# TensorE's table reads in the routed tiles of a fused Mamba and mixture-of-experts kernel: one per tile, ahead of the down products, the weight offset computed

## The reference

```
scores = softmax(x @ gate_w.T)            # 16 experts
topk_w, topk_ids = top_k(scores, 6)       # normalised to sum 1
y_e = (silu(x @ g_e.T) * (x @ u_e.T)) @ w2_e.T      # hidden 352
out = sum over the six chosen e of weight * y_e, + shared expert (hidden 704)
x = x + tanh(g_ffn) * out
```

## Time and profile before

| | us |
|---|---|
| median of three runs | 1439.65 |
| lowest and highest run | 1438.64, 1913.43 |
| span of the profiled execution, first to last instruction | 1435.5 |
| median less that span | 4.15 |
| TensorE products busy | 1349.9 (94%) |
| GpSimd busy | 949.3 (66%) |
| VectorE busy | 787.5 (55%) |
| ScalarE busy | 730.9 (51%) |

### The profile page before, as it was taken

The page is one execution under the profiler, slowest core; times in us unless marked ns, Lnnn a source line. Parts: engine busy times, 40 slices in busy tenths (PEclk is TensorE's granted clock), DMA queues, the critical chain, the costliest instruction groups (busy, mean ns, idle before and its releaser), DMA issues.

```text
span 1435.5 us, 32257 instructions
## 1 busy us (share of the span) xinstructions
PE 1349.9 (94%) x8480; PEld 1210.6 (84%) x8481; DVE 787.5 (55%) x1364; ACT 730.9 (51%) x1317; POOL 949.3 (66%) x671
## 2 busy tenths in 40 slices
PE   6897998997898899999999999999999999999996
PEld 2686887887888799999998989989889988899885
DVE  6878898898989854653333333333333333333331
ACT  5898897898889464343332333323333333332321
POOL 0588898898988747887456665566645666546632
PEclk8899999999999999999999999999999999999999
DMA  4120122222242365645455435555445544454432
GB/s 137 38 74 31 53 67 96 67 73 91 75 146 72 133 129 106 142 84 141 83 141 145 131 63 144 139 147 137 104 94 137 141 135 104 95 147 131 76 68 36
DMA packets 65042, 149.13 MB, mean 104 GB/s; under 512 B 16976, under 2 KB 17616, under 8 KB 62656
## 3 DMA queue, kind: packets, MB, share of 16 engines
q0 software_dynamic: 31024, 62.10, 22.9%
q1 hardware_dynamic: 33392, 81.21, 17.5%
q10 hardware_dynamic: 560, 4.98, 1.0%
HBM read 101.50 MB, written 48.99 MB: 105 GB/s over the span
## 4 chain that ended last, share of the span: by engine, by line
PE 65%; DVE 3%; issue 1%; POOL 0%; ACT 0%; DVEq 0%; POOLq 0%; ACTq 0%
PE bank L1719 19%; PE bank L1699 19%; PE bank L1700 18%; PE bank L1687 3%; PE bank L1710 3%; DVE hs L1172 1%; PE bank L1604 1%; PE bank L1590 1%; PE bank L1602 0%; POOL hc L949 0%; DVE sc L1226 0%; PE bank L1665 0%; DVEq L1375 0%; DVE xl L1363 0%; DVE du L1186 0%
## 5 line engine op out<-in xcount | busy, mean ns | idle before, releaser
L949 POOL TENSOR_TENSOR hc<-hs,crow 128x512 f32<-128x512 f32 x254 | 322.6, 1302 | 91.8 <-DVE hs L1172 84.6
L1699 PE MATMUL bank<-w,xh 128*128 (+1 forms) x1088 | 368.7, 340 | 7.6 <-issue 4.2
L1015 POOL DMA_INDIRECT out_x<-ys,aid x104 | 171.2, 1646 | 275.0 <-issue 215.7
L1700 PE MATMUL bank<-w,xh 128*128 (+1 forms) x1088 | 351.2, 323 | 0.0
L1172 DVE TENSOR_TENSOR_SCAN hs<-dA,bank 128x512 f32<-128x512 f32 x256 | 295.8, 1208 | 47.9 <-PE bank L1604 32.0
L1719 PE MATMUL bank<-w,ah 128*128 (+1 forms) x816 | 264.7, 405 | 2.7 <-DVE al L1399 2.7
L1399 DVE TENSOR_TENSOR al<-bank,ah 128x384 fp32r<-128x384 f32 x136 | 75.8, 557 | 331.0 <-ACT ah L862 283.2
L1699 PEld LDWEIGHTS bank<-w,xh 128*128 128x128 f32 x1088 | 204.3, 188 | 35.9 <-issue 32.1
L1700 PEld LDWEIGHTS bank<-w,xh 128*128 128x128 f32 x1088 | 206.4, 190 | 2.3
L868 ACT COPY ys<-bank 128x512 f32<-128x512 f32 x136 | 79.9, 587 | 195.9 <-PE bank L1719 191.5
L1700 PE MATMUL bank<-w,xl 128*128 (+1 forms) x544 | 175.9, 323 | 0.0
(11 more groups left out here) (184 smaller groups left out, 2051.7 us busy)
## 6 DMA issues: line engine op xcount, KB each, us to landing
wraw<-in_wall SPq DMA_DIRECT2D x16, 2176.0 KB
crow<-c_rows SPq DMA_DIRECT2D x64, 256.0 KB, 3.3
xt<-token_rows_turned SPq DMA_DIRECT2D x32, 256.0 KB
out_x<-ys POOLq DMA_DIRECT2D x32, 256.0 KB
wraw<-in_wall ACTq DMA_DIRECT2D x2, 2176.0 KB
token_rows<-rowb SPq DMA_DIRECT2D x4, 1028.0 KB
xrow<-in_x SPq DMA_DIRECT2D x4, 1024.0 KB, 7.0
out_x<-xrow SPq DMA_DIRECT2D x4, 1024.0 KB, 4.9
```

The lines of the kernel that those rows point to most:

```text
L949: nc.gpsimd.tensor_tensor(hc[:, j, :], hs[:, j, :], crow[:, n % 4, :], ALU.mult).then_inc(hc_done, 1)
L1015: pool.indirect_dma_start(out_rows, bass.IndirectOffsetOnAxis(ap=aid[:, s:s + 1], axis=0), ys[:, s, :], None, bounds_check=TOKENS - 1, oob ...
L1699: nc.tensor.matmul(gate_bank[:, 0:I], xx, columns(w, off + ww + k * 2 * I, I), start=first, stop=last)
L1700: mm = nc.tensor.matmul(up_bank[:, 0:I], xx, columns(w, off + ww + k * 2 * I + I, I), start=first, stop=last)
```

## The change

TensorE reads only row 0 of the table. For the second, third and fourth tile of a turn, the read stands at the end of the tile before, between `turn_x` and `down`; for the first tile of a turn it stands at the turn's head, together with a read of the number of the tile before. The offset is worked out in registers from the number: `(number + 1) % 2 * (2 * WCOLS)`, once for each tile of the turn and once for the tile before it. The wait for `wl_done` stays ahead of the up products. Reads of the table by TensorE go from nine to five per turn. The last tile, outside the loop, is treated in the same way.

```diff
-            def weights_of(t):
-                needed = pe.value_load(meta[0:1, 0, bass.ds(t, 1)], min_val=1, max_val=NX)
-                apart(pe, wl_done, needed, "pe")
-                return pe.value_load(meta[0:1, 1, bass.ds(t, 1)], min_val=0, max_val=2 * WCOLS)
-
-            def tile(t, s4, old, off, more=True, m=None):
+            def set_number(t):
+                return pe.value_load(meta[0:1, 0, bass.ds(t, 1)], min_val=1, max_val=NX)
+
+            def offset_of(number):
+                return pe.snap((number + 1) % 2 * (2 * WCOLS))
+
+            def tile(t, s4, old, off, more=True, m=None, ahead=None):
...
                     turn_x(t + 1, (s4 + 1) % 4, m)
-                down(t - 1, 1 - s, old() if callable(old) else old)
+                number = set_number(ahead) if ahead is not None else None
+                down(t - 1, 1 - s, old)
+                return number
...
             with pe.Fori(0, groups) as i:
-                def old():
-                    return pe.value_load(meta[0:1, 1, bass.ds(4 * i + PEELED - 1, 1)], min_val=0, max_val=2 * WCOLS)
-
+                number = set_number(4 * i + PEELED)
+                old = offset_of(set_number(4 * i + PEELED - 1))
                 for k in range(4):
-                    off = weights_of(4 * i + PEELED + k)
-                    tile(4 * i + PEELED + k, (3 + k) % 4, old, off, True, i)
+                    off = offset_of(number)
+                    apart(pe, wl_done, number, "pe")
+                    number = tile(4 * i + PEELED + k, (3 + k) % 4, old, off, True, i, 4 * i + PEELED + k + 1 if k < 3 else None)
                     old = off
             last = tiles_but_12(pe) + 11
-
-            def of_last(k):
-                return pe.value_load(meta[0:1, 1, bass.ds(last - k, 1)], min_val=0, max_val=2 * WCOLS)
-
-            tile(last, 3, lambda: of_last(1), weights_of(last), False)
+            number = set_number(last)
+            old, off = offset_of(set_number(last - 1)), offset_of(number)
+            apart(pe, wl_done, number, "pe")
+            tile(last, 3, old, off, False)
             turn_a(last, 1)
-            down(last, 1, of_last(0))
+            down(last, 1, off)
```

## The result

The changed kernel takes 1430.89 us in the median of five runs (1428.72 to 1434.58), the kernel before 1438.64 in five; the ratio is 0.9947, 95% interval 0.9934 to 0.9959. That is 0.5% faster, some 7.7 us, where 1443, slower by 3, was forecast, in a range that began at 1433. A second measurement of the same code (the first experiment) gives 0.9962, 0.9948 to 0.9975. One run of the kernel before, 1913.43, counts in its median and not in the ratio.

The account below looks back on a forecast made before the run. TensorE was taken to bound the routed stage, with 20.3 us of pauses at tile boundaries. Terms: -9.0 inner boundaries, +11.3 turn heads, +1.0 slower reads, sum +3.3 us, time 1443; range 1433 to 1453.

Parts of the forecast that it names:

- The bound and the pool: Routed stage: TensorE sets the pace; its pauses at 104 tile boundaries hold 20.3 us, all that can be won there.
- the 15 late tiles: Tiles where ScalarE and VectorE also split the next weights and activations come late; said to hold 10.3 of 20.3 us.
- (a): 78 inner boundaries: two reads give way to one computed offset; 9.0 us won, between 7.6 and 13.0.
- (b): Read moved ahead of the down products: costs nothing, taking 0.7 to 1.4 of 2.4 us in which the sequencer waits.
- The queue's fill: TensorE's queue behind the moved read; the only ground given for R3.
- (c): Head of each turn, 27 times: two computed offsets added on the path, 0.42 us each time, 11.3 us lost (6.5 to 20.5).
- (d): Loop turns: with inner gaps closed, about six more turns have a first read slowed by the gather; 1.0 us lost.
- R1: Rival: inner gaps close wholly, 13.0 us won, offsets cheap at 6.5 + 1.0 paid; 1434 us, chance 0.22.
- R2: Rival: at the turn's head each offset takes three or four instructions; 13.5 us slower, 1453 us, chance 0.20.
- R3: Rival: the moved read isn't hidden and delays down products by some 0.4 us in 78 tiles; 1474 us, chance 0.03.
- R4: Rival: late xl, not the reads, ended the gaps everywhere; inner boundaries win 2 instead of 9, 1450 us, chance 0.05.
- the case that had 0.95: Whole kernel: measured time the same within about 2% (29 us); faster had 0.01, slower 0.04.

Follow-up runs that it names:

- the first experiment: The changed kernel measured again with no edit: 1432.35 us, ratio 0.9962 to the kernel before.
- both reads ahead: Kernel before, with both reads of the next tile (number and table offset) moved ahead of the down products: 1437.54 us, ratio 1.0003.
- three inner reads: Changed kernel with three more set-number reads at each inner boundary, between down products and the next tile's up products: 1465.99 us, ratio 1.0195.
- the extra reads in the slot: Changed kernel with each read ahead of the down products made twice, 78 reads more: 1433.08 us, ratio 0.9975.
- the old offset in the slot: Changed kernel with the old offset's read put back just ahead of the down products of a turn's first tile: 1425.51 us, ratio 0.9918.

## Why the prediction was wrong

**The bound and the pool: right.** The pauses at tile boundaries come from TensorE's sequencer and hold about 20 us; the experiments take out 18 of them. The row shown for a late tile is of a loop turn, since the loop's branch stands there between the down addresses and the read:

```profile
L1759 PEldq COMPARE_BRANCH  x1: 215/215/215, 1022.7 to 1022.7; - x1
```

Four of the 15 late tiles are turns; the sum of 10.3 us over the 15 is right.

**(a) The inner boundaries: right in mechanism, and with some luck in size.** 9.0 forecast, 9.2 measured, but the 9.0 was picked between 7.6 and 13.0. What stays is the late low part of x, as said; putting it first takes the inner rest from 6.0 to 0.6. It shows on the chip what the row with L1363 as releaser had shown.

**(b) The read ahead of the down products costs nothing: right for this change, and for two reads; I had the slot too wide.** I read 2.4 us off one tile, and that one is beside a weight split, where the activations come late. Over the tiles of the loop, from the wait for the gathered rows to the first down address, it is 1.4 to 2.9 us, 1.7 in the median, and a third read in it costs 0.29 us. The queue's fill was counted wrong as well: at 1019.4 the trace has 17 products and 16 loads still to start ahead of the down products, 33 and not 56.

**(c) The head of the turn: the step that failed, and it decided.** The two computed offsets were to cost 0.42 us a turn, 11.3 in all, with 6.5 as the low bound. It is the term that turned the sign of the sum. Measured: the turns' excess rises by 3.0 to 3.6, and (d) has its part in that. The offset is no instruction of its own; it is folded into the register instruction that makes the address of the product that uses it, +62 ns for the new one (42 to 104) on the path. The old one is folded into the down products' first address (46 to 119 ns), which lies in the slot. So it is one 0.06 and not two 0.21: 26 x 0.06 = 1.6 us. The run with both reads ahead says the same from outside, 0.9 to 1.5. The turns' mean of 0.94 to 0.97 us lies between the 0.6 to 0.8 that I had named as the sign of (c) being wrong and the 1.0 to 1.25 of its being right. My nearest row was ScalarE's 114 ns; I took it as a whole instruction added, with a space behind it, when that row too was the address instruction of the operation, of which only what exceeds the usual 46 is the arithmetic. I had named the merging as a bound and still priced it at 0.12.

**(d) The turns' luck: right in kind.** The first read at the head has 358 ns in the mean of 25 turns before, 400 to 420 after, slow in 14 turns for 8: 26 x 0.04 to 0.06 = 1.1 to 1.6 us, 1.0 forecast. By the run with both reads ahead it is 2.1, and with three inner reads the loss turns round, as the gaps do; how far beyond the reads' own length it goes stays open. Its cause was put down to the gather alone, which doesn't hold.

The sum with (c) at its size: -9.2 + 1.6 + 1.4 = -6.2, against the 1438.64 of the measurement 1432.4; the two measurements are 1430.9 and 1432.4. The number is near that of R1, to which I gave 0.22, but not by its parts: R1 had the gap closing wholly (13.0) and 6.5 paid for the offsets; it was 9.2 and at most 1.6, below even the low bound. R2 is refuted by the 104 ns, R3 by the extra reads in the slot, R4 by the 34 pauses gone. The ratio is within 2%, the case that had 0.95.

## What to carry to other kernels

Price a sequencer's instruction by its place: the same table read cost nothing in the slot, nothing at an inner boundary, and 0.65 us at the head of the loop. What counts at a place is the whole way to the next issue against the work that is still queued, and against whatever that issue has to wait for anyway. A computed value that feeds an address may cost only the growth of the address instruction; look at what such an instruction takes without it before pricing it with it. And count what else shares the slot that you move work into, in its fullest position and not in a typical one: three reads in the slot of one tile in four gave back the whole gain of all the boundaries.

## What the runs showed of the hardware

A read of the table from SBUF into a sequencer's register takes 273 ns at least on ScalarE, 283 on GpSimd, 295 on TensorE and 297 on VectorE, and 278 to 308 in the median (kernel before). Slow ones of 960 to 1010 ns stand in that trace on TensorE, VectorE and GpSimd, and one of 950 on ScalarE in that of the old offset in the slot; in the kernel before they go with a DMA share of GpSimd's queue of 0.94 for 0.35. From one read on TensorE to the next, with the checks between, it is 0.64 us where the address is the same, 0.75 where it has to be worked out (1053.3 to 1054.05, both reads ahead). The remainder, the addition and the multiplication of this offset fold into one register instruction with the address, for 62 ns more on the up address (42 to 104) and 73 on the down address (46 to 119).
